# Making one low one-hot half in eight on GpSimd, between its gathers, in a graph attention aggregate

## What is computed

```python
e = leaky_relu(a_src[src] + a_dst[dst], 0.2)          # one score per edge and head
ee = exp(e - segment_max(e, dst)[dst])
alpha = ee / segment_sum(ee, dst)[dst]
msgs = xp[src] * alpha[:, :, None]                    # xp = (h @ W) as (N, 4, 256)
out = segment_sum(msgs, dst)                          # the weighted aggregate
...
agg = segment_sum(h[edge_src], edge_dst)              # the two later layers: unweighted
out = h @ W_self + (agg * deg_inv[:, None]) @ W_neigh + b
```

## Time and profile before

| | |
|---|---|
| median of 3 runs | 3783.8 us (3776.98 to 3787.24) |
| profiled execution, its own time | 3771.5 us |
| its span, first to last instruction | 3769.9 us |
| weighted aggregate, first gather to last product | about 665 to 1396 us |
| granted clock of PE, whole span | 0.934 |

### The profile page before, as it was taken

One profiled execution on the slowest core, in us unless ns is written; L12 is line 12 of the kernel. 1 busy time (PEld: TensorE's weight loads), 2 busy tenths in 40 slices (PEclk: granted clock), 3 DMA queues, 4 the chain that ended last, 5 costly groups with the idle time before them and its releaser, 6 DMA issues. The chain is left out here.

```text
span 3769.9 us, 73085 instructions
## 1 busy us (share of the span) xinstructions
PE 3009.6 (80%) x20638; PEld 1728.3 (46%) x20638; DVE 2407.2 (64%) x4226; ACT 1175.1 (31%) x2623; POOL 1714.0 (45%) x1809
## 2 busy tenths in 40 slices
PE   0668887588999970049999998799699999997999
PEld 0435553477888860024444443344244444442454
DVE  7749886899999987845555555433355656555222
ACT  3643352477777863320000000133300000000111
POOL 5003222477777753345655656300166656665000
PEclk9889988799999995579999999999899999998999
DMA  2659993588888867779998999533499999997333
GB/s 72 199 178 350 320 350 94 179 305 294 302 307 294 306 214 248 246 238 322 311 311 303 323 302 309 180 92 92 156 304 335 346 322 332 344 331 272 87 87 87
DMA packets 289506, 946.76 MB, mean 251 GB/s; under 512 B 57726, under 2 KB 58730, under 8 KB 289424
## 3 DMA queue, kind: packets, MB, share of 16 engines
q0 software_dynamic: 224848, 726.45, 56.3%
q1 hardware_dynamic: 64576, 219.26, 18.4%
HBM read 905.16 MB, written 130.57 MB: 275 GB/s over the span
## 5 line engine op out<-in xcount | busy, mean ns | idle before, releaser
L1425 POOL DMA_INDIRECT agg_got<-h_rows,agg_idx_now x896 | 902.1, 1007 | 538.4 <-PE agg_sum_ps L1559 329.9
L1559 PE MATMUL agg_sum_ps<-agg_got,agg_hot 128*128 128x512 f16 x3584 | 855.4, 382 | 106.1 <-DVE sum_acc L1478 66.3
L1478 DVE TENSOR_TENSOR sum_acc<-agg_sum_ps,sum_acc 125x1024 f32 x448 | 548.1, 1223 | 608.0 <-PE agg_sum_ps L1559 540.9
L1543 PE MATMUL gagg_sum_ps<-gagg_got,gagg_hot_hi 128*128 128x256 f16 x3584 | 602.4, 273 | 119.7 <-ACT gagg_hot_hi L1516 35.5
L1516 ACT ACTIVATE gagg_hot_hi<-gagg_hot,gat_high_e 128x128 f16<-128x128 f16 x1792 | 547.7, 388 | 197.6 <-DVE gagg_hot L1448 197.6
L1425 POOL DMA_INDIRECT gagg_got<-xs_rows,gagg_idx_now x448 | 508.3, 1135 | 200.7 <-issue 104.0
L1559 PEld LDWEIGHTS agg_sum_ps<-agg_got,agg_hot 128*128 128x128 bf16 x3584 | 338.1, 98 | 561.1 <-issue 172.5
L915 PE MATMUL agg_out_ps<-agg_w,agg_a_t 128*128 128x512 f16 x2400 | 566.9, 379 | 0.0
L804 PE MATMUL neigh_out_ps<-neigh_w,neigh_a_t 128*128 128x512 f16 x2400 | 529.2, 381 | 8.4 <-DMA neigh_w<-split_w 8.4
L1543 PE MATMUL gagg_sum_ps<-gagg_got,gagg_hot_lo 128*128 128x256 f16 x1792 | 490.1, 273 | 0.0
L895 ACT ACTIVATE agg_a_t<-agg_turn_ps 128x2048 f16<-128x2048 f16 x50 | 93.8, 1877 | 1231.4 <-PE agg_turn_ps L903 1231.4
(11 more groups left out here) (254 smaller groups left out, 2834.1 us busy)
## 6 DMA issues: line engine op xcount, KB each, us to landing
edg_piece<-slot_rows POOLq DMA_DIRECT2D x56, 512.0 KB
agg_a<-h_rows SPq DMA_DIRECT2D x50, 448.0 KB
part_rows<-agg_rows SPq DMA_DIRECT2D x50, 448.0 KB
neigh_rows<-part_rows SPq DMA_DIRECT2D x50, 448.0 KB
edg_w_buf<-in_L_gnn_W_self_dram SPq DMA_DIRECT2D x32, 512.0 KB, 8.2
edg_w_buf<-in_L_gnn_W_neigh_dram SPq DMA_DIRECT2D x32, 512.0 KB, 10.9
split_w<-edg_w_out SPq DMA_DIRECT2D x32, 512.0 KB, 8.6
agg_got<-h_rows,agg_idx_now POOLq DMA_INDIRECT x896, 7.2
```

Source lines behind the costliest of these rows:

```text
L1425: g.indirect_dma_start(out=got[:, k, :], out_offset=None, in_=rows_in[:, :], in_offset=bass.IndirectOffsetOnAxis(ap=idx_now[:, s, k:k + 1] ...
L1478: v.tensor_tensor(acc[:, tl, :], sum_ps[n % 2][0:TN, :].rearrange("p (a d) -> p a d", a=1), acc[:, tl, :], ALU.add).then_inc(added, 1)
L1543: t.matmul(sum_ps[n % 2][:, h * C:(h + 1) * C], hot_k[:, u % HOTS, h, :], got[:, u % R, part * D + h * C:part * D + (h + 1) * C], start=(u ...
L1559: last = t.matmul(sum_ps[n % 2][:, q * HALF:(q + 1) * HALF], hot[:, u % HOTS, :], got[:, u % R, cols], start=(u == steps[0] and part == 0) ...
```

## The change

In the weighted aggregate the low half of every eighth chunk, that with slot 7, is made by POOL and not by DVE. POOL does it after the gather of slot 4 of the next group: the gathers of slots 0 to 4 of that group, then the product for chunk 7 of the group before, then the gathers of slots 5 to 7. The product of the very last group stands behind POOL's loop. It has a semaphore of its own, `eighth_lo_ready`, for which PE waits ahead of every pair with chunk 7; the counts of `hot_lo_ready` are now seven in eight. So that the first group can leave the product out, the first round of POOL's loop is written out, for all three aggregates.

```diff
@@ block.gpsimd
-                    with g.Fori(0, ROUNDS) as i:
+                    def low(i, u):
+                        s = B * i + u
+                        g.wait_ge(hot_ready, s + 1)
+                        g.wait_ge(mm_done, s + 1)
+                        g.tensor_tensor(hot_lo[:, u % HOTS, :, :], hot[:, u % HOTS:u % HOTS + 1, :].to_broadcast([P, H, P]),
+                                        weight_e[:, ds(s, 1), 1, 0:H].rearrange("p a h -> p (a h)").unsqueeze(2).to_broadcast([P, H, P]),
+                                        ALU.mult).then_inc(eighth_lo_ready, 1)
+                    def round_(i, first):
                         for s in range(B // R):
...
+                                if weighted and k == 4 and not (first and s == 0):
+                                    u = R * s + k - 5
+                                    low(i if u >= 0 else i - 1, u % B)
+                    round_(0, True)
+                    with g.Fori(1, ROUNDS) as i:
+                        round_(i, False)
+                    if weighted:
+                        low(ROUNDS - 1, B - 1)
@@ block.vector, make_hots
                             for u in range(PAIR * n, PAIR * (n + 1)):
+                                if u % 8 == 7:
+                                    continue
@@ block.tensor, round_
-                                t.wait_ge(hot_lo_ready, B * i + PAIR * (n + 1))
+                                t.wait_ge(hot_lo_ready, B // 8 * 7 * i + (PAIR * (n + 1) - (n + 1) // 4))
+                                if n % 4 == 3:
+                                    t.wait_ge(eighth_lo_ready, B // 8 * i + (n + 1) // 4)
```

More of the change, by code:

```diff
@@ L1403, in aggregate @@
                 idx_ready, hot_ready, hot_hi_ready, hot_lo_ready = sem("idx_ready"), sem("hot_ready"), sem("hot_hi_ready"), sem("hot_lo_ready")
+                eighth_lo_ready = sem("eighth_lo_ready")
                 arrived = [sem(f"arrived{k}") for k in range(R)]
```

## The result

| | before | after |
|---|---|---|
| median (lowest to highest) | 3780.4 us (3766.7 to 3787.2) | 4011.1 us (3999.5 to 4014.8) |
| profiled execution, its own time | 3771.5 | 3999.5 |
| weighted aggregate, its whole stretch | 731 us | 957 us |

The changed kernel is slower: after over before is **1.0605** [1.0584, 1.0626], 231 us. The forecast was 4053 us, +7.1% of 3783.8. Its direction, its place and its mechanism were right, and the time lies in the range; the size came out some 40 us too large.

A forecast was written before the change was run, and what follows sets the result against it. POOL's own chain was taken to fill the 12.34 us group; 14.73 + 0.6 (meeting DVE) + 1.9 (clock) = 17.23 us, so 55 x 4.89 = +269 on 3771.5, plus 12.3, gives 4053 us. Range 3895 to 4130 us.

The forecast's parts named there:

- What bounds the kernel: Weighted aggregate: POOL's own chain of gathers and index copy fills the 12.34 us group; DVE close at 11.7 us.
- The relief of DVE: One low half in eight off DVE: 39 us less busy, gaining between 0 and 1.1 us a group through shorter gathers.
- The product's own length: POOL's added 128x512 product, 56 times: 1.10 us each, with 1.0 to 1.3 as ends.
- The wait: PE's pair with chunk 7 waits for slot 4's gather, then the product; group's chain 14.73 us before meeting and clock.
- The meeting of the product with DVE's low halves: POOL's product meets DVE's next two low halves and waits 0.6 us, making the group 15.3 us.
- The clock: PE idles 4.4 us a group; half clock costs the first pair 2.1 us in nine groups of ten, +1.9 us.
- The other edits: Changed PE waits and written-out first rounds of every aggregate: 0, at most a few us for fetching new code.
- The signs it named: Some 55 PE idle pieces of 4 to 5 us, copies 17 us apart, clock near 0.85, later aggregates unchanged.
- POOL's own time alone: Rival: PE's wait vanishes as POOL runs ahead; only 1.10 to 1.8 us a group added, 3844 to 3883; chance 0.06.
- The clock holds: Rival: PE's idle piece doesn't lower the clock; 15.3 us a group, +165, 3949 (3879 to 3985); chance 0.28.
- Worse: Rival: DVE's two-input work keeps the product out longer than one pair of low halves; above 4130; chance 0.05.
- Faster: Rival: the product fits POOL's idle time and gathers shrink to 0.99 us; -69, 3715; chance 0.03.

The follow-up runs named there:

- experiment 9: Kernel before the change, with POOL's index copy for the next group moved behind the gather of slot 4, in all three aggregates: 3745.7 us, 0.9925.
- experiment 2: Changed kernel without POOL's product: DVE makes seven low halves of eight, nobody the eighth, whose slot holds zeros: 3766.9 us, 0.9972 of the kernel before.
- experiment 1: Changed kernel with POOL's product written to an unread buffer; DVE makes all low halves, PE doesn't wait for POOL: 3820.5 us, 1.0116 of the kernel before.
- experiment 3: Changed kernel with POOL's product moved from behind the gather of slot 4 to behind that of slot 1: 3807.5 us, 1.0081 of the kernel before.
- experiment 4: Changed kernel with POOL's product moved from behind the gather of slot 4 to behind that of slot 3: 3869.6 us, 1.0243 of the kernel before.
- experiment 6: Changed kernel with 30 unread filler products on PE ahead of its wait for POOL's low half: 3923.8 us, 1.0382 of the kernel before.
- experiment 5: Changed kernel with 16 unread filler products on PE ahead of its wait for POOL's low half: 3949.6 us, 1.0454 of the kernel before.
- experiment 10: Changed kernel with POOL's product behind the gather of slot 1 and the next group's indices copied behind that of slot 4: 3752.5 us, 0.9937.
- experiment 7: Changed kernel where DVE makes all low halves and POOL, instead of the product, only counts up the semaphore PE waits for: 3778.8 us, 1.0009.

## Why the prediction was right, and where it was off

**What bounds the kernel: confirmed, with DVE close behind.** That POOL's own chain fills the period is borne out by experiment 9 (shorten it with DVE's work unchanged, and the period is 0.2 us shorter) and by experiment 2 (take 0.69 us a group off DVE, and only the 0.2 us come by which the gathers shrink). Experiment 1 lengthens POOL's chain by 0.9 us and the period by as much, but DVE is busy for 99% of it there.

**The relief of DVE: confirmed.** Taken as nothing on the path, with at most 1.1 us a group; alone it is 10 us in all, 0.2 us a group (experiment 2).

**The product's own length: confirmed.** 1.10 was taken, 1.0 to 1.3 given; it is 1.05, and 1.41 at the most.

**The wait: confirmed as a mechanism, and nearly in size.** Experiment 3 shows it by moving the product alone: some 200 of 231 us go. The chain, step by step, from the gather of slot 4 at 1004.96 to the next at 1020.14:

| step | predicted | measured, full clock |
|---|---|---|
| gather, product, release of PE | 2.19 | 2.21 |
| pair with chunk 7 | 2.72 | 2.87 |
| PE's end to the gather of slot 6 | 0.74 | 0.74 |
| gathers of slots 6 and 7 | 2.28 | 2.78 |
| copy, and the time behind it | 1.08 | 1.08 |
| gathers of slots 0 to 3 | 5.72 | 5.50 |
| product held by DVE | 0.6 | 0 |
| sum | 15.3 | 15.2 |

The sum came out so near by luck as well: the 0.6 us of the product's meeting and the 0.22 in the gathers of slots 0 to 3 were too much, the 0.50 in the gathers of slots 6 and 7 and the 0.15 in the pair too little. The 2.72 us were read from the end of one pair to the end of the next; the pairs of the kernel before overlap by 0.14, and one that starts behind a gap counts from its own start, 2.86. POOL's lag behind PE at the gather of slot 4 was given as 1.66 us and is 1.93 in this group; as experiment 4 shows, it is this lag, and not the condition of that gather, that opens the gap.

**The meeting of the product with DVE's low halves came out the other way round.** The prediction had the product wait 0.6 us for DVE. It does meet them, but in 54 of 56 groups it lasts 1.05 us, and in 25 of them the first low half of a pair, begun some 0.54 us ahead of the product, is the one that is drawn out:

```profile
1020.62 2.15 DVE L1476 TENSOR_TENSOR gagg_hot_lo<-gagg_hot,gat_weight_e 128x512 f16<-128x512 f16 x1
...
1022.69 0.68 DVE L1476 TENSOR_TENSOR gagg_hot_lo<-gagg_hot,gat_weight_e 128x512 f16<-128x512 f16 x1
```

The first takes 2.15 us for 0.69, with POOL's product from 1021.16 to 1022.21 in it, and the pair 2.75 for 1.29: 1.05 of the 1.46 us are the product's, and the rest has no row. The low half ends 0.56 us behind the product, so it can have done little of its 0.69 us of work before. DVE has room in the changed kernel (731 of 957 us), so this costs nothing. In its place the gather of slot 7 meets DVE's next pair and takes 1.48 us, which the prediction had at 0.99.

The section that the prediction cites has it that the instruction which issues later is blocked for the whole of the other's (the Trainium skill, "SBUF — State Buffer", section "Who interferes with whom"). That the two exclude each other agrees with these rows; the order does not, as far as the starts in the profile tell it: the low half begins first and is the one that waits. Two products of the 56, begun 0.17 us behind a low half, did take 1.41 us. What decides between the two cases no run shows. The same section has it that a tensor_tensor of VectorE was not seen to hold up the issue of DMAs; the gathers of 1.41 to 1.48 us inside low halves, here and in experiment 9, speak against this once more.

**The clock: the right term, too large.** The prediction had 2.1 us in nine groups of ten, +1.9 us. Measured: a half-clock pair takes 4.6 for 2.86 us, so 1.76, in 41 of 52 groups, +1.4 us. With the 15.0 to 15.1 us that groups at full clock take on average (experiments 6 and 5) that gives the 16.5 us of the trace. Experiment 6 gives the same from the other side: 76 us / 55 = 1.4 us a group, 1.5 by the periods (16.5 against 15.0). The 2.1 lay between bounds of 1.6 and 2.7. What came is near the lower one, from the piece of 2.98 us; the piece of 3.99 us and the stage's first pair, behind 24.75 us of idle time, had pulled the value up, though the length of 4 us is the nearer one.

That a gap between stretches of products lowers the clock anew every time (the Trainium skill, "TensorE: Matmul & The Clock Gate", section "HAM oscillation — how this bites in real kernels") is seen in four groups of five.

**The sum.** 17.23 us a group was predicted, 16.48 measured: 0.5 too much in the clock and 0.3 in the chain (15.33 for 15.0), 0.75 x 55 = 41 us. That is the whole miss. The other edits were put at nothing, and new code at a few us at most, for which no row stood: outside the stage the two profiled executions differ by 2 us in sum.

**The signs it named** all came: 55 pieces of PE's idle time named after POOL's low half (222.3 us, 4.04 on average; 4 to 5 were given), POOL idle for 2.6 to 3.9 us ahead of the gather of slot 6, copies 16.5 us apart (17 given), a clock of 0.89 (0.85 given), later aggregates unchanged.

**The rivals.** "POOL's own time alone" (3844 to 3883) is refuted by the waits, and experiment 1 puts its price lower, at 3820. The argument against it, that the wait of the gather of slot 4 forbids POOL to run ahead, was not the reason: in experiment 4 PE waits without it. "The clock holds" (3949) holds for 11 groups of 52, and for all but one in experiment 6. "Worse" needed the product to be kept out by DVE, which it wasn't. "Faster" is refuted twice: the most that the relief is worth is 10 us, and POOL's gaps of 0.30 us can take no work.

## What to carry to other kernels

Before work is given to an engine that looks idle, find out what else stands in its list ahead of the new instruction, and who will wait for it: here the same product cost 231 us behind the fifth gather, 93 behind the fourth and 30 behind the second, and nothing in the busy shares of the kernel before tells these three apart. Price the relief first by leaving the work out (10 us here): if that is less than the operation costs where nobody waits for it (44 us), a better place is unlikely to save the change, and none of the three places tried here did. A gap of a few us per round on TensorE costs its own length, less what TensorE had to spare, and then often more than half a pair's time again through the clock (1.76 of 2.86 us here), and fillers are a quick way to tell the two apart.

## What the runs showed that was not expected

- **A piece of 2 us can be enough to lose the clock.** In experiment 5 a piece of 2.08 us was followed by a half-clock pair, and so were 14 of 25 at 2.0 to 2.3 us, but none of the 24 shorter ones; in the changed kernel it was 41 of 52 at 3.65 us and above. The length of one piece alone doesn't decide it: in experiment 4 all four pieces of about 2.1 us, each right behind a group with a half-clock pair, lost the clock, all 20 of about 2.45 us kept it, and in the changed kernel 3.76 us left it at 1.00.
- **Gathers fall in and out of step with VectorE.** Whether a gather takes 0.99 or 1.44 us depends on whether it starts inside a low half, so each change of the period changes their mean, between 1.07 and 1.20 us in these kernels. In experiment 9 this took back three quarters of the gain, in experiments 3 and 10 it paid for part of the product.
- **A semaphore counted up by POOL's sequencer doesn't wait for the gathers ahead of it** (experiment 7: PE was released 0.8 us before the gather began that the count stands behind).
- **One chip of three took 3.5% longer for the same kernel** (3909.8 against 3774 to 3777 us), with counts of PE that reach POOL and DVE up to 2.4 us late at some pairs. There is no trace of the kernel before from that chip, so this is read from the two kernels that ran on it, and its cause is open.
